# Pairs in turn in banded attention, raw weights in two waves, and stack stores on ScalarE in a two-layer transformer kernel

## What is computed

```python
x = L0_attn_a_x                                    # (2, 1024, 128)
x = x + attn_a(_layernorm(x), Wq, bq, Wk, bk, ...) # 16 heads of 8, softmax over all 1024 keys
x = x + ffn(_layernorm(x), gate_w, ...)            # 64 experts of 64, best 6 of the best 4 groups, 2 shared
x = x + attn_b(_layernorm(x), ...)                 # 16 heads of 8, key j only if i - 31 <= j <= i
x = x + ffn(_layernorm(x), gate_w, ...)            # the same expert weights
```

## Time and profile before

| | |
|---|---|
| median of 3 runs | 1168.04 us (1163.45 to 1170.56) |
| profiled execution | 1164.44 us, its span 1162.6 us |
| TensorE matmul busy | 1046.3 us (90%) |
| VectorE busy | 927.4 us (80%) |
| ScalarE busy | 706.3 us (61%) |
| GpSimd busy | 461.6 us (40%) |
| start, to the first score product | 0 to 42 us |
| full attention with its output part | to 427 us |
| first expert layer | to 716 us |
| banded attention with routing | to 882 us |
| second expert layer | to the end |

### The profile page before, as it was taken

One profiled execution on the slowest core, in us unless ns is written; L12 is line 12 of the kernel. 1 busy time (PEld: TensorE's weight loads), 2 busy tenths in 40 slices (PEclk: granted clock), 3 DMA queues, 4 the chain that ended last, 5 costly groups with the idle time before them and its releaser, 6 DMA issues. The chain is left out here.

```text
span 1162.6 us, 18837 instructions
## 1 busy us (share of the span) xinstructions
PE 1046.3 (90%) x6308; PEld 425.8 (37%) x6308; DVE 927.4 (80%) x2139; ACT 706.3 (61%) x1083; POOL 461.6 (40%) x434
## 2 busy tenths in 40 slices
PE   5669999999999979999999996777888999999997
PEld 4212222222222325444445442333434544444443
DVE  8588999999998467889788776765775879877775
ACT  2445878777777765666656663444455566666664
POOL 4116246433100105565554553100112566555554
PEclk8657999999999989999999998688979999999999
DMA  8411303311200126666765981122205667687662
GB/s 306 112 36 29 79 2 78 79 45 35 54 2 1 42 74 162 164 175 175 194 164 150 223 195 40 51 70 74 74 3 143 159 153 187 173 196 202 186 186 57
DMA packets 72185, 131.63 MB, mean 113 GB/s; under 512 B 12680, under 2 KB 47624, under 8 KB 72088
## 3 DMA queue, kind: packets, MB, share of 16 engines
q1 hardware_dynamic: 69600, 122.50, 40.9%
q10 hardware_dynamic: 2488, 7.93, 1.9%
HBM read 115.08 MB, written 14.91 MB: 112 GB/s over the span
## 5 line engine op out<-in xcount | busy, mean ns | idle before, releaser
L419 ACT ACTIVATE Aatt_prob<-Aatt_st 128x1024 f32<-128x1024 f32 x256 | 247.7, 1022 | 73.3 <-PE Aatt_st L314 72.3
L485 DVE TENSOR_REDUCE Aatt_mx<-Aatt_sc 128x1 f32<-128x512 f32 x451 | 280.6, 683 | 12.0 <-PE Aatt_sc L301 11.5
L1980 POOL TENSOR_TENSOR M1ex_low<-M1ex_hid,M1ex_high 128x512 f16<-128x512 f32 x132 | 152.7, 1157 | 135.9 <-ACT M1ex_high L1879 68.4
L1980 POOL TENSOR_TENSOR M2ex_low<-M2ex_hid,M2ex_high 128x512 f16<-128x512 f32 x132 | 152.7, 1157 | 129.6 <-PE M2ex_acc L1835 72.1
L301 PE MATMUL Aatt_sc<-ks,qs 48*128 48x512 bf16 x496 | 152.9, 408 | 33.9 <-DMA ks<-stack 11.2
L1873 ACT ACTIVATE M2ex_sil<-M2ex_ring,unscale 128x512 f32<-128x512 f32 x132 | 90.7, 687 | 92.4 <-PE M2ex_ring L1818 92.1
L1873 ACT ACTIVATE M1ex_sil<-M1ex_ring,unscale 128x512 f32<-128x512 f32 x132 | 90.7, 687 | 90.2 <-PE M1ex_ring L1818 89.7
L325 PE MATMUL Aatt_pv<-Aatt_prob,vg 128*32 128x512 f32 x1024 | 138.5, 613 | 0.6 <-ACT Aatt_prob L419 0.6
L1917 DVE SCALAR_TENSOR_TENSOR M2ex_ring<-M2ex_ring,unscale,M2ex_sil 128x512 f32<-128x512 f32 x132 | 100.0, 758 | 39.9 <-ACT M2ex_sil L1873 39.3
L1917 DVE SCALAR_TENSOR_TENSOR M1ex_ring<-M1ex_ring,unscale,M1ex_sil 128x512 f32<-128x512 f32 x132 | 99.9, 757 | 37.0 <-ACT M1ex_sil L1873 33.7
L301 PEld LDWEIGHTS Aatt_sc<-ks,qs 48*128 48x128 bf16 x496 | 35.9, 93 | 206.3 <-DVE Aatt_mx L485 171.4
(11 more groups left out here) (433 smaller groups left out, 1922.8 us busy)
## 6 DMA issues: line engine op xcount, KB each, us to landing
M1ex_cb<-comb SPq DMA_DIRECT2D x130, 256.0 KB, 4.1
M2ex_cb<-comb SPq DMA_DIRECT2D x130, 256.0 KB, 4.1
M_wt<-wsplit SPq DMA_DIRECT2D x132, 192.0 KB, 4.0
wsplit<-split_cut SPq DMA_DIRECT2D x9, 704.0 KB, 4.5
qs<-stack SPq DMA_DIRECT2D x32, 96.0 KB
ks<-stack SPq DMA_DIRECT2D x30, 96.0 KB
split_raw<-in_wg_dram ACTq DMA_DIRECT2D x3, 704.0 KB, 8.3
split_raw<-in_wu_dram ACTq DMA_DIRECT2D x3, 704.0 KB, 13.2
```

Of the source, the lines that this page charges most:

```text
L419: act.activation(prob[e % 4][:, :, :].rearrange("p a c -> p (a c)"), st[pr][:, :, :].rearrange("p a c -> p (a c)"), ACT.Exp, scale=SCALE). ...
L485: ins = dve.tensor_reduce(mx[k][:, m, h:h + 1], scores, AX.X, ALU.max)
L1980: pool.tensor_tensor(low[q % 3][:, :], hid[q % 3][:, :], high[q % 3][:, :], ALU.subtract).then_inc(low_ready, 1)
```

## The change

Five edits. The banded `scores` takes one pair: both heads of it one after the other, behind that pair's wait; in a step, pair 0's scores stand between the mask products and the transposed products, pair 1's where all four stood. Batch 1's stack stores move from SyncE's stage to ScalarE's side work, one in each slot. The raw weights come in two waves: pieces 0 to 2 where all nine were issued, 3 to 8 behind ScalarE's loads of group 0; `TOPS` takes piece 3 out of the start and puts it to 4 to 8. Group 0's two stores count on a semaphore of their own, and its loads wait for that alone. In the full attention, group 0's maxima are transposed in the bank of the value products, so that neither the transpose nor tile 4 waits for the other.

```diff
         def turn_bank(n):
-            return sc[bank_index(n + 1, TURN_TILE)][:, :].bitcast(BF16)[0:3 * HG * TB, 0:P]
+            bank = sc[bank_index(n + 1, TURN_TILE)] if n else pv
+            return bank[:, :].bitcast(BF16)[0:3 * HG * TB, 0:P]
...
-                if i == TURN_TILE and n:
+                if i == TURN_TILE and n > 1:
                     pe.wait_ge(m_copied, n)
...
                 if kc == 0:
                     pe.wait_ge(u_out, ONE + n * 2 + qh)
+                    pe.wait_ge(m_copied, 1)
...
                     if n == 1 and 4 * blk == TURN_TILE:
-                        turn_max(0, 0, True)
+                        turn_max(0, 0, False)
...
             largest(0, 0)
-            split_tops(dve, weights, 3)
+            split_tops(dve, weights, 2)
...
-                if n + 3 == G:
-                    store_stacks(sp, env, v2, 1)
...
-            def scores(n, k, qt):
+            def scores(n, k, qt, pr):
 
                 first = 0 if qt else WIN
+                rows = slice(HALF * pr, HALF * pr + MAXROW)
+                pe.wait_ge(red_done, n * 2 * STEPS + 2 * qt + pr + 1)
                 for h in range(2):
-                    for pr in range(2):
-                        if h == 0:
-                            pe.wait_ge(red_done, n * 2 * STEPS + 2 * qt + pr + 1)
-                        rows = slice(HALF * pr, HALF * pr + MAXROW)
-                        mm = pe.matmul(sc[pr][:, h * BAND + first:(h + 1) * BAND], qs[k][rows, h, qt * P:(qt + 1) * P],
-                                       ks[k][rows, h, qt * P - WIN + first:(qt + 1) * P], start=True, stop=True)
-                        if h == 1:
-                            mm.then_inc(sc_done, 1)
+                    mm = pe.matmul(sc[pr][:, h * BAND + first:(h + 1) * BAND], qs[k][rows, h, qt * P:(qt + 1) * P],
+                                   ks[k][rows, h, qt * P - WIN + first:(qt + 1) * P], start=True, stop=True)
+                mm.then_inc(sc_done, 1)
...
                         pe.matmul(st[pr][:, :], env.ident16[:, :], mask_k[:, :], start=True, stop=True)
+                    blocks = score_blocks(s, k, nxt, nxt2)
+                    for off, kk, qt in blocks:
+                        scores(n + off, kk, qt, 0)
...
                     next(beside, None)
-                    for off, kk, qt in score_blocks(s, k, nxt, nxt2):
-                        scores(n + off, kk, qt)
+                    for off, kk, qt in blocks:
+                        scores(n + off, kk, qt, 1)
...
                 yield from qkv_scalar(act, env, v2, bank, 1)
+                for i in range(2):
+                    act.wait_ge(v2.low_ready, 2 * i + 2)
+                    act.wait_ge(v2.mid_ready, 2 * i + 2)
+                    for g in range(G):
+                        act.dma_start(env.stack[i, G + g].rearrange("s r t -> r s t"),
+                                      v2.part[32 * g:32 * g + 32, i, :, :]).then_inc(env.stored[1], 16)
+                        yield
...
-            store_stacks(sp, env, v, 0, (0,))
-            sp.wait_ge(env.stored[0], STORES)
+            store_stacks(sp, env, v, 0, (0,), first_stored)
+            sp.wait_ge(first_stored, 32)
             load_half_group(sp, 0)
+            sp.wait_ge(env.stored[0], STORES - 32)
...
-            split_load(act, env.weights)
+            split_load(act, env.weights, 0)
             rest_of(norm_of_batch_scalar(act, env, n, bank))
             rest_of(qkv_scalar(act, env, v, bank, 0))
-            store_stacks(act, env, v, 0, (1,))
+            store_stacks(act, env, v, 0, (1,), first_stored)
             act.wait_ge(keys_set, 2)
-            act.wait_ge(env.stored[0], STORES)
+            act.wait_ge(first_stored, 32)
             load_half_group(act, 1)
+            split_load(act, env.weights, 1)
...
-            split_tops(dve, env.weights, 2)
...
-TOPS = ((0, 1), (2,), (3,), (4, 5, 6, 7, 8))
+WAVES = ((0, 1, 2), (3, 4, 5, 6, 7, 8))
+TOPS = ((0, 1), (2,), (3, 4, 5, 6, 7, 8))
...
-def split_load(sp, w):
-
-    for q, (i, j) in enumerate(PIECES):
+def split_load(sp, w, wave):
+
+    for q in WAVES[wave]:
+        i, j = PIECES[q]
         sp.dma_start(w.raw[q][:, :, :], w.sources[i][:, j:j + PIECE, :]).then_inc(w.raw_in[q], 16)
```

More of the change, by code:

```diff
@@ L703, in _ @@
                 for qt in range(STEPS if n == 0 else AHEAD):
-                    scores(n, n, qt)
+                    for pr in range(2):
+                        scores(n, n, qt, pr)
                 if n == 0:
@@ L856, in start @@
         sem = lambda n: semaphore(nc, env, f"start_{n}")
-        x_in, x1_in, projections_in, loaded, made, ones_set, keys_set, biased = map(sem, (
-            "x_in", "x1_in", "projections_in", "loaded", "made", "ones_set", "keys_set", "biased"))
+        x_in, x1_in, projections_in, loaded, made, ones_set, keys_set, biased, first_stored = map(sem, (
+            "x_in", "x1_in", "projections_in", "loaded", "made", "ones_set", "keys_set", "biased", "first_stored"))
         bank = side_banks(nc, ctx, "start")
@@ L1649, in qkv_scalar, with store_stacks @@
     yield
-def store_stacks(sp, env, v, b, which=(0, 1)):
+def store_stacks(sp, env, v, b, which=(0, 1), first_stored=None):
     for i in which:
@@ L1658, in store_stacks @@
             sp.dma_start(env.stack[i, b * G + g].rearrange("s r t -> r s t"),
-                         v.part[32 * g:32 * g + 32, i, :, :]).then_inc(env.stored[b], 16)
+                         v.part[32 * g:32 * g + 32, i, :, :]).then_inc(
+                             first_stored if first_stored and g == 0 else env.stored[b], 16)
 def qkv_vector(dve, env, v, bank, b, lows=True):
```

## The result

| | before | changed |
|---|---|---|
| median of 20 runs each | 1164.42 us (1162.20 to 1170.56) | 1160.42 us (1148.67 to 1165.58) |
| ratio, 95% interval | | 0.9949 [0.9925, 0.9972] |
| profiled execution, span | 1164.44, 1162.6 | 1157.54, 1155.7 |
| mean granted clock of the profiled execution | 0.937 | 0.932 |

The account below looks back on a forecast made before the run. Open were the start, waiting for loads, and the banded attention, where nothing was near full. From 1164.4 us, -8.0 + 1.2 - 7.4 + 1.3 = -12.9 gives 1151.5, forecast 1153.3; range 1145 to 1162.

Parts of the forecast that it names:

- Start: Kernel start: raw weights in two waves and loads waiting only for group 0's stores bring the first score 8.0 us sooner.
- the upper row, 8.6: Group 0's loads at the start: 8.6 us in the profile before, the slower of two rows behind the assumed 8.0.
- +1.2: Full attention after group 0's scores: one more weight maximum, less the waits saved by moving the transpose, costs 1.2 us.
- Score phase in pairs: Banded attention, group 0 and group 1's ahead blocks: pairs in turn stop VectorE idling, blocks about 1.23 us, -4.0 us.
- Pairs in a step: Banded attention steps: one pair's products lose overlap, costing 0.27 us at 1.2 GHz, 0.13 at 2.4; fast steps net 0.0.
- every step pays: Rival, banded attention: 39 fast steps also lose 0.13 us each, +5.1 us, giving 1158.4; chance 0.17.
- Stores on ScalarE: Banded attention: earlier stack stores bring group 4's load sooner, -7.4 us including earlier banded terms; a 1.3 us stall stays.
- Behind it: Banded attention after the stall for group 4's load: five slow steps pay 0.27 us each, +1.3 us.
- the clock helps: Rival, full and banded attention: shorter TensorE idling raises the granted clock, gaining 4.6 and 1.2 us, giving 1147.5; chance 0.15.
- the second wave: Rival, start: second-wave raw weights take the loads' bandwidth, gain 1.2 instead of 8.0 us, giving 1160.1; chance 0.12.
- The 1.8 us added for the three runs' median: Whole kernel: the median of three runs lay 3.6 us above the profiled execution; half was added, 1151.5 becoming 1153.3.
- The 0.65 for faster by over 1%: Whole kernel: chance 0.65 of a time below 1156.4 us, from nearly all the forecast and the clock rival.

Follow-up runs that it names:

- e8: e4 with ScalarE issuing the second wave of raw weights behind its share of the second batch's norm, some 4.5 us later; 1150.89 us, ratio 0.9878.
- e5: Changed kernel with a step's score products back behind the transposed products, pair 0's two and then pair 1's two; 1154.23 us, ratio 0.9915.
- e2: Kernel before with only the pairs in turn in the banded attention, in group 0's score phase and in the steps; 1166.03 us, ratio 0.9998.
- e7: e4 with useless products added ahead of the first score, behind each pair's scores and ahead of the transpose of group 0's maxima; 1155.69 us, ratio 0.9921.
- e4: Changed kernel with the steps' score products in the old order and place, pairs in turn only in the score phase; 1149.92 us, ratio 0.9869.
- e11: e4 with ten useless products at the end of group 3 of the banded attention; 1151.20 us, ratio 0.9902.

## Why the prediction was right, and where it was not

- **Start.** Right in mechanism: loads issued at 26.14 (26.2), the next block at 33.84 (33.0), six maxima in 9.24 us (9.25). Mis-sized: the loads' 8.0 us, which were 9.9. They lie above the upper row, 8.6. The other six stores are a part of the reason at most: in the changed kernel's trace the last packets of stores start before 28, under 2 us into the loads, and in 30 to 32 of e8, with neither stores nor raw weights moving, the loads had 84 GB/s. Why they are that slow stays open. -6.4 instead of -8.0. What follows to the first exponentials cost +0.7 where +1.2 was said.
- **Score phase in pairs.** Right: TensorE's blocks follow each other every 1.21 us, and the first mask comes 3.8 us sooner against the stage's start (4.0).
- **Pairs in a step.** The term of 0.27 and 0.13 us a step failed in its reasoning. I priced the four score products as neighbours of one pair. In the profile above, the score products start within 0.01 us of transposed products (724.87 and 724.88, 724.98 twice, 725.25 and 725.24): eight products in the time of four, 724.87 to 725.59, 0.72 us. Before, with the pairs alternating all the way, the eight took 0.73 (740.64 to 741.37):

```profile
740.64 0.45 PE L727 MATMUL Batt_st<-qs,ks 51*128 51x160 bf16 x4
740.88 0.49 PE L660 MATMUL Batt_sc<-ks,qs 48*128 48x160 bf16 x4
```

  A transposed product, which the program has behind both of pair 0's score products, starts at 724.88, ahead of the second of them at 724.98. That fits pair 0 and pair 1 each running its own four in program order, side by side. e5 shows it without transposed products between, pair 0's two and then pair 1's two in the time of two at the high clock:

```profile
800.71 0.32 PE L658 MATMUL Batt_sc<-ks,qs 48*128 48x160 bf16 x4
```

  I had taken neighbours in the program for neighbours in time. A slow step is 2.0 us as before (728.16 to 730.16). The Trainium skill (TensorE: Matmul & The Clock Gate, "Part 3: Packing small matmuls") lets small products of different row groups overlap; the trace agrees. The rival "every step pays" fell with it: at the high clock the changed kernel's steps last 1.61 us where before had 1.58, not 1.71.
- **Stores on ScalarE.** The number is right to 0.1 us, -7.4 up to group 2's step 4, and the stores do free the load, the last one issued at 763.26. But that the number fits is in part luck, by two errors that cancel. The stall is gone altogether, where 1.3 us was left in the sum, because TensorE came later on its own: group 0's eight steps took 21.2 us instead of 18.6, its last two 4.3 and 4.7 us instead of 2.5 and 3.7, at a granted clock of 0.56 over the group instead of 0.70. Changed, then before:

```profile
724.20:745.45 21.25, 20.73 (x166) 9.45 (x166) 15.60 (x99) 8.74 (x21) 2.55 (x5) 0.56 0.17 47
735.66:754.24 18.58, 17.88 (x167) 7.38 (x166) 15.68 (x101) 8.80 (x21) 2.54 (x5) 0.70 0.16 46
```

- **Behind it.** This is the step that failed: +1.3 was said, the profile shows +6.0, and +2.1 more in the second expert layer. It was worked out at the clock of before. The clock was not that of before: over 32 runs the changed kernel has 0.9304, over 62 runs the one before has 0.9388, and 0.0084 by 6.6 us per 0.01 is 5.6 us. At a clock of 0.945 the changed kernel's fit gives 1149.6 and that of before 1163.3 (slope -3.0 per 0.01, correlation only -0.54, since its clock varies little), 13.7 us apart; with the changed kernel's slope for both it is 11.5. The sum's 12.9 lies between, though not since each term was right: the start gave 1.6 us less, and the 3.4 us for pairs in the steps were not paid. The term that was missing was the clock's own answer to the new order, with the sign against "the clock helps".
- **The forecast as a whole.** 1160.4 lies in the range, but 7 us from the forecast, and that the range held it is luck: its upper end was there for two rivals, the second wave and "every step pays", and neither came true. The 1.8 us added for the three runs' median were not there: over 20 runs the median before is 1164.42, the profiled execution's own time. The 0.65 for faster by over 1% was too much: that side held only if the granted clock stayed, and the only rival about the clock had one sign.

Left open: why pair 0's products ahead of the transposed ones lower the mean clock, and why five or ten useless products near a group's end, at either of two places, raise it again. Shown is that they do (18 runs against 32), that both profiles of the changed kernel lose it at the same places, and that the pauses at group 3's end do not by themselves decide it (e2 and e7). That the clock's answer is a matter of TensorE's load in the microseconds ahead is only argued, and e7 speaks against the simple form "busy keeps it high".

## What to carry to other kernels

Where a stage's time hangs on the granted clock, cost an edit at one clock, and give the clock a term of its own with both signs; then read each execution's time against its mean clock before blaming the work. Split an edit by places: in the score phase the new order brought the first mask product 3.8 us sooner, in the steps it cost 10.5 us of the median. When a cure works, run it once at a place where it shouldn't, and look in the profiles of the other experiments for the supposed cause without its effect.

## What the runs showed of the hardware that was not expected

- The changed kernel's 32 executions spread from 1148.67 to 1165.58 us, and time follows the mean granted clock (0.948 to 0.918) with a correlation of -0.93.
- The granted clock fell to its low level at 718 us in e7 when TensorE had been busy for 7 us, after idling in the 2.5 us before that. In the changed kernel it stayed at 0.50 from 798 to 810, though TensorE was busy for all 12.00 of these 12 us.
- Useless products of 0.13 us each made the changed kernel faster: ten of them 1160 to 1151 us (in e4's step they gave nothing, e11).
- Eight small products of two pairs took 0.72 us, the time of four, although two score products of one pair follow one another in the program; one of pair 1's, later in the program, started ahead of pair 0's second.
- Group 0's loads, 0.79 MB, took 9.9 us with the second wave issued 2.8 us behind them and 9.7 us with it issued 5.0 us behind.
